# Two graph layers on one core: one-hots from 32-bit lanes, 32-bit rows in the first layer, sums cleared by ScalarE

## The reference, cut to what matters

```python
deg_inv_sqrt = jnp.where(deg > 0, jax.lax.rsqrt(jnp.maximum(deg, 1.0)), 0.0)
out = jax.ops.segment_sum(x[row] * (deg_inv_sqrt[row] * deg_inv_sqrt[col])[:, None], col, num_segments=n)
x = _layernorm(x + out)                       # first layer
h = jax.nn.relu(edge_feat @ W1 + b1)          # 212500 x 64
w = (h @ W2 + b2).reshape(e, 4, 8, 8)
m0 = ALPHA * (s_e*sh0 with w_000  +  C110 * v_e.sh1 with w_110)
m1 = ALPHA * (s_e*sh1 with w_011  +  v_e*sh0 with w_101)
x = _layernorm(x + segment_sum([m0, m1], dst) + SI_SCALE * self_interaction(x))   # second layer
```

## Time and profile before

| | us |
|---|---|
| median of 3 runs | 4708.02 |
| the profiled execution | 4711.18 |
| its span, first to last instruction | 4709.2 |
| PE busy | 2447.2 (52%) |
| PEld busy | 1661.3 (35%) |
| DVE busy | 2178.6 (46%) |
| ACT busy | 795.4 (17%) |
| POOL busy | 3317.1 (70%) |

### The profile page before, as it was taken

The page is one execution under the profiler, slowest core; times in us unless marked ns, Lnnn a source line. Parts: engine busy times, 40 slices in busy tenths (PEclk is TensorE's granted clock), DMA queues, the critical chain, the costliest instruction groups (busy, mean ns, idle before and its releaser), DMA issues.

```text
span 4709.2 us, 30989 instructions
## 1 busy us (share of the span) xinstructions
PE 2447.2 (52%) x10122; PEld 1661.3 (35%) x10122; DVE 2178.6 (46%) x2299; ACT 795.4 (17%) x772; POOL 3317.1 (70%) x3353
## 2 busy tenths in 40 slices
PE   6112122221212212122178888888888888888886
PEld 5111111111111111111165555555555555555555
DVE  8300000000000000000048888888888888888884
ACT  0000000000000000000013333333333333333331
POOL 0577777777777777777727777777777777777770
PEclk7555555555555555555558989999989989899996
DMA  1111111111111111111101111111111111111110
GB/s 34 31 19 19 19 19 19 19 19 19 19 19 19 19 19 19 19 19 19 24 19 29 26 28 29 26 29 28 27 29 26 29 29 26 28 29 26 29 29 16
DMA packets 170010, 112.08 MB, mean 24 GB/s; under 512 B 100473, under 2 KB 154250, under 8 KB 169775
## 3 DMA queue, kind: packets, MB, share of 16 engines
q0 software_dynamic: 106528, 68.39, 10.0%
q1 hardware_dynamic: 63345, 41.87, 3.2%
HBM read 104.41 MB, written 5.61 MB: 23 GB/s over the span
## 4 chain that ended last, share of the span: by engine, by line
POOL 45%; PE 19%; issue 17%; DVE 10%; DMA 7%; ACT 1%; POOLq 0%; DVEq 0%; SPq 0%; ACTq 0%
POOL yg L344 45%; PE ps L477 12%; DMA yg<-scaled_x_table,idx 5%; PE ps L556 4%; DVE msg L899 4%; PE ps L506 2%; DMA yg<-x_table,idx 2%; PE ps L454 1%; DVE prod_all L889 1%; DVE oh L747 1%; DVE prod_all L883 1%; DVE z_sb L645 1%; ACT vec L401 1%; PE ps L549 1%; DVE msg L908 0%
## 5 line engine op out<-in xcount | busy, mean ns | idle before, releaser
L344 POOL DMA_INDIRECT yg<-scaled_x_table,idx x1664 | 1671.5, 1004 | 657.4 <-issue 530.9
L344 POOL DMA_INDIRECT yg<-x_table,idx x1664 | 1635.0, 983 | 612.7 <-issue 520.6
L477 PE MATMUL ps<-oh,yg 128*96 128x144 bf16 x1664 | 455.7, 442 | 1784.8 <-DMA yg<-scaled_x_table,idx 1784.8
L556 PE MATMUL ps<-w2t,hT 128*128 128x256 f32 x3328 | 956.4, 437 | 366.6 <-ACT hT L392 366.6
L760 DVE TENSOR_TENSOR sumT_all<-sumT_all,ps 96x144 f32 (+1 forms) x208 | 61.1, 294 | 2041.3 <-PE ps L477 2041.3
L477 PEld LDWEIGHTS ps<-oh,yg 128*96 128x96 bf16 x1664 | 284.4, 178 | 1955.9 <-DMA yg<-scaled_x_table,idx 1838.4
L556 PEld LDWEIGHTS ps<-w2t,hT 128*128 128x128 f32 x3328 | 673.2, 213 | 803.2 <-ACT hT L392 542.5
L899 DVE TENSOR_REDUCE msg<-prod_all 128x192 f32<-128x1536 f32 x416 | 723.9, 1740 | 0.0
L883 DVE TENSOR_TENSOR prod_all<-ps,feat 128x768 f32<-128x768 f32 x416 | 397.4, 955 | 342.1 <-PE ps L556 275.0
L477 PE MATMUL ps<-ohf,msg 128*64 128x144 f32 x3328 | 473.4, 305 | 8.5 <-DVE msg L908 8.5
L477 PEld LDWEIGHTS ps<-ohf,msg 128*64 128x64 f32 x3328 | 442.2, 148 | 71.2 <-issue 58.6
(11 more groups left out here) (99 smaller groups left out, 705.1 us busy)
## 6 DMA issues: line engine op xcount, KB each, us to landing
yg<-scaled_x_table,idx POOLq DMA_INDIRECT x1664, 2.4
efT<-in_efT SPq DMA_DIRECT2D x104, 256.0 KB
yg<-x_table,idx POOLq DMA_INDIRECT x1664
idx<-in_src SPq DMA_DIRECT2D x208, 8.0 KB, 1.6
sh<-in_sh SPq DMA_DIRECT2D x104, 32.0 KB
scaled_x_table<-sumT_all SPq DMA_DIRECT2D x4, 588.0 KB
x_sb<-in_x SPq DMA_DIRECT2D x1, 1568.0 KB
x_table<-q_sb SPq DMA_DIRECT2D x8, 196.0 KB
```

What stands on the lines that cost most here:

```text
L344: pool.indirect_dma_start(rows[k][:, t, :], None, table, bass.IndirectOffsetOnAxis(ap=idx[k][:, t:t + 1], axis=0),).then_inc(s_g[layer][k] ...
L477: mm = pe.matmul(ps_sum[layer][:, k, :], rows[:, t, :], oh[k][:, :, t] if layer == 0 else ohf[:, t, :], start=(t == 0), stop=(t == TPC - 1))
L556: mm = pe.matmul(ps_w[j % 2][:, t, :], hT[j % 2][:, t * P:(t + 1) * P], w2t[:].rearrange("p c o i -> p (c o i)"), start=True, stop=True)
```

## The change

The split in three parts is dropped. VectorE scales the rows once per quarter, and the table holds 32 values of 32 bits (`y_d`); the gathered rows go to the same buffers in both layers (`xg`), and the first layer's matmuls are 32-bit as the second's. The sum of a chunk is made in two spans of 8 tiles (`SPC`, `TPS`), each 76 lanes wide (`SW`) and with a base of its own, so that the one-hots are 16 x 76 32-bit values from the 32-bit lanes `lane_f` in both layers, and are read by TensorE as they are: ScalarE's conversion (408) goes. `load_bases` reads two registers and `add_sums` makes two additions of 76 columns, the second waiting for the first. ScalarE clears the sums in both layers (`clear_sums`), from a constant zero, in place of VectorE's memsets. In the second layer ScalarE's scalars come after the second rectification, not the first. POOL's warm-up gather and the small identities `parts` are gone.

```diff
@@ -15,8 +15,9 @@
-LW = 144
-D3 = 96
+SPC = 2
+TPS = TPC // SPC
+SW = 76
@@ -62,7 +63,7 @@
-        y_d = nc.dram_tensor("scaled_x_table", (NPAD, D3), BF16).ap()
+        y_d = nc.dram_tensor("scaled_x_table", (NPAD, D), F32).ap()
@@ -70,8 +71,7 @@
-        sumT = [sumT_all[0:D3, :], sumT_all[0:DM, :]]
-        y3 = sumT_all[:, 0:NC * D3 // 2].bitcast(BF16).rearrange("p (c f) -> p c f", f=D3)
+        sumT = [sumT_all[0:D, :], sumT_all[0:DM, :]]
@@ -122,22 +121,18 @@
-        yg = [sb(f"yg{k}", [P, TPC, D3], BF16) for k in range(2)]
-        xg = [yg[k][:].rearrange("p t f -> p (t f)").bitcast(F32)[:, 0:TPC * D].rearrange("p (t f) -> p t f", f=D)
-              for k in range(2)]
+        xg = [sb(f"xg{k}", [P, TPC, D]) for k in range(2)]
...
-        oh = [sb(f"oh{k}", [P, LW, TPC], BF16) for k in range(2)]
-        ohf = sb("ohf", [P, TPC, LW])
+        oh_all = [sb(f"oh{k}", [P, TPC, SW]) for k in range(2)]
+        oh = [[o[:] for o in oh_all]] * 2
...
-        wide_all = prod[0].rearrange("p t b i o -> p (t b i o)")
-        wide_oh = [wide_all[:, 0:WIDE].bitcast(BF16).rearrange("p (t w) -> p t w", t=2),
-                   wide_all[:, 0:2 * WIDE].rearrange("p (t w) -> p t w", t=2)]
+        wide_oh = [prod[0].rearrange("p t b i o -> p (t b i o)")[:, 0:2 * WIDE].rearrange("p (t w) -> p t w", t=2)] * 2
@@ -146,8 +141,8 @@
-        ps_sum = [ps[0:m, 6:8, 0:LW] for m in (D3, DM)]
-        ps_wide = [ps[0:m, 7, :] for m in (D3, DM)]
+        ps_sum = [ps[0:m, 6:8, 0:SPC * SW].rearrange("p k (s w) -> p k s w", s=SPC) for m in (D, DM)]
+        ps_wide = [ps[0:m, 7, :] for m in (D, DM)]
@@ -238,9 +232,9 @@
-                sp.wait_ge(s_split[0], 3 * q + 3)
+                sp.wait_ge(s_scaled, q + 1)
...
-                sp.dma_start(y_v[:, c, :], y3[0:NP, c, :]).then_inc(s_table[0], 16)
+                sp.dma_start(y_v[:, c, :], z_sb[0:NP, c, :]).then_inc(s_table[0], 16)
@@ -320,11 +309,6 @@
-            pool.wait_ge(s_idx[0][0], 16)
-            pool.indirect_dma_start(xg[0][:, 0, :], None, x_d,
-                                    bass.IndirectOffsetOnAxis(ap=idx[0][:, 0:1], axis=0)).then_inc(s_warm, 16)
-            pool.wait_ge(s_warm, 16)
@@ -357,12 +341,13 @@
         def _(act):
...
             act.activation(root[0:NP, :], root[0:NP, :], ACT.Sqrt).then_inc(s_root, 1)
-            for q in range(SPLITS):
-                c = slice(q * SC, (q + 1) * SC)
-                for part in range(2):
-                    act.wait_ge(s_split[0], 3 * q + part + 1)
-                    act.activation(y3[0:NP, c, D * part:D * (part + 1)], z_sb[0:NP, c, :],
-                                   ACT.Copy).then_inc(s_split[1], 1)
+            def clear_sums(layer):
+                act.activation(sumT[layer], zero_b[0:sumT[layer].shape[0], 0:1].to_broadcast([sumT[layer].shape[0], SUMW]),
+                               ACT.Copy).then_inc(s_zero, 1)
...
+            act.wait_ge(s_pool_c, 11)
+            act.wait_ge(s_degree, 1)
+            clear_sums(0)
@@ -401,29 +386,14 @@
                                xg[k][:, :, MUL:D].rearrange("p t (i m) -> p t i m", m=3), ACT.Copy).then_inc(s_scal, 1)
...
-            def one_hots_f32(n):
-                act.wait_ge(s_oh[1], n + 1)
-                if n >= 1:
-                    act.wait_ge(s_sum[1], n)
-                act.activation(ohf[:].rearrange("p t w -> p w t"), oh[n % 2][:], ACT.Copy).then_inc(s_ohf, 1)
...
-            act.wait_ge(s_near, 1)
-            all_near = act.value_load(near[0:1, 0:1], min_val=0, max_val=1)
...
-            def rectified(near_sums):
-                for n in range(CHUNKS):
-                    rectify(GPC * n)
-                    scalars(n)
-                    rectify(GPC * n + 1)
-                    rectify(GPC * n + 2)
-                    rectify(GPC * n + 3)
-                    if near_sums:
-                        one_hots_f32(n)
...
-            with act.If(all_near == 1):
-                rectified(True)
-            with act.Else():
-                rectified(False)
+            act.wait_ge(s_tr[0], PIECES)
+            clear_sums(1)
+            for n in range(CHUNKS):
+                rectify(GPC * n)
+                rectify(GPC * n + 1)
+                scalars(n)
+                rectify(GPC * n + 2)
+                rectify(GPC * n + 3)
@@ -467,15 +437,14 @@
                 k = n % 2
...
-                    pe.wait_ge(s_oh[0], n + 1)
                 else:
                     pe.wait_ge(s_msg, 2 * n + 2)
-                    pe.wait_ge(s_ohf, n + 1)
+                pe.wait_ge(s_oh[layer], n + 1)
...
-                    pe.wait_ge(s_acc[layer], n - 1)
+                    pe.wait_ge(s_acc[layer], SPC * (n - 1))
...
-                    mm = pe.matmul(ps_sum[layer][:, k, :], rows[:, t, :], oh[k][:, :, t] if layer == 0 else ohf[:, t, :],
-                                   start=(t == 0), stop=(t == TPC - 1))
+                    mm = pe.matmul(ps_sum[layer][:, k, t // TPS, :], rows[:, t, :], oh[layer][k][:, t, :],
+                                   start=(t % TPS == 0), stop=(t % TPS == TPS - 1))
                 mm.then_inc(s_sum[layer], 1)
...
             def wide_sums(layer, rows, n, landed):
@@ -497,26 +466,26 @@
-                pe.wait_ge(s_acc[layer], CHUNKS)
+                pe.wait_ge(s_acc[layer], SPC * CHUNKS)
...
                     for c in range(CPP):
...
-                                       parts[0:D3, :] if layer == 0 else places[0:DM, :], start=True, stop=True)
+                                       ident[0:D, 0:D] if layer == 0 else places[0:DM, :], start=True, stop=True)
...
-                    window_sums(0, yg[n % 2], n)
+                    window_sums(0, xg[n % 2], n)
...
-                    wide_sums(0, yg[k], k, (k, 16 * TPC))
+                    wide_sums(0, xg[k], k, (k, 16 * TPC))
...
-                        wide_sums(0, yg[k], 2 * i + k, (k, 16 * TPC * i + 16 * TPC))
+                        wide_sums(0, xg[k], 2 * i + k, (k, 16 * TPC * i + 16 * TPC))
@@ -599,25 +568,25 @@
-            dve.tensor_copy(first_f[:], first_i[:, ::GPC]).then_inc(s_dve_c, 1)
+            dve.tensor_copy(first_f[:], first_i[:, ::GPC // SPC]).then_inc(s_dve_c, 1)
...
-            step(dve.tensor_tensor(rel.rearrange("p (n t) -> p n t", t=TPC),
-                                   dst_f[:].rearrange("p (n t) -> p n t", t=TPC),
-                                   first_f[:].unsqueeze(2).to_broadcast([P, CHUNKS, TPC]), ALU.subtract))
+            step(dve.tensor_tensor(rel.rearrange("p (n t) -> p n t", t=TPS),
+                                   dst_f[:].rearrange("p (n t) -> p n t", t=TPS),
+                                   first_f[:].unsqueeze(2).to_broadcast([P, CHUNKS * SPC, TPS]), ALU.subtract))
...
-            step(dve.tensor_copy(lane[:], lane_f[:, 0:LW].unsqueeze(2).to_broadcast([P, LW, TPC])))
+            step(dve.tensor_copy(lane[:], lane_f[:, 0:NC].unsqueeze(2).to_broadcast([P, NC, TPC])))
...
-            step(dve.tensor_scalar(near_f[:, 0:1], spans[:, 0:1], LW - 0.5, None, ALU.is_le))
+            step(dve.tensor_scalar(near_f[:, 0:1], spans[:, 0:1], SW - 0.5, None, ALU.is_le))
@@ -703,23 +672,10 @@
             dve.wait_ge(s_xin, 16)
...
-            def scaled(q):
+            for q in range(SPLITS):
...
-                                  dinv[0:NP, c].unsqueeze(2).to_broadcast([NP, SC, D]),
-                                  ALU.mult).then_inc(s_split[0], 1)
...
-            def scaled_rest(q, part):
-                c = slice(q * SC, (q + 1) * SC)
-                dve.wait_ge(s_split[1], 2 * q + part + 1)
-                out = z_sb[0:NP, c, :] if part == 0 else y3[0:NP, c, 2 * D:3 * D]
-                dve.tensor_tensor(out, z_sb[0:NP, c, :], y3[0:NP, c, D * part:D * (part + 1)],
-                                  ALU.subtract).then_inc(s_split[0], 1)
...
-            for q in range(SPLITS):
-                scaled(q)
-                for part in range(2):
-                    scaled_rest(q, part)
+                                  dinv[0:NP, c].unsqueeze(2).to_broadcast([NP, SC, D]), ALU.mult).then_inc(s_scaled, 1)
@@ -743,22 +699,25 @@
             def one_hots(layer, n):
                 k = n % 2
...
-                    dve.wait_ge(s_sum[0] if layer == 0 else s_ohf, n - 1)
-                dve.tensor_tensor(oh[k][:], rel_b[:, n * TPC:(n + 1) * TPC].unsqueeze(1).to_broadcast([P, LW, TPC]),
-                                  lane[:], ALU.is_equal).then_inc(s_oh[layer], 1)
...
-            def load_base(n):
...
-                return dve.value_load(first_i[0:1, GPC * n:GPC * n + 1], min_val=0, max_val=n_out)
...
-            def add_sums(layer, n, base):
+                    dve.wait_ge(s_sum[layer], n - 1)
+                dve.tensor_tensor(oh[layer][k], rel_b[:, n * TPC:(n + 1) * TPC].unsqueeze(2).to_broadcast([P, TPC, SW]),
+                                  lane_f[:, 0:SW].unsqueeze(1).to_broadcast([P, TPC, SW]),
+                                  ALU.is_equal).then_inc(s_oh[layer], 1)
...
```

(25 more changed lines are left out.)

36 lines of the change are left out of this document (14 added, 22 removed).

## The result

The changed kernel takes 4665.9 us (median of 4 runs, 4665.0 to 4667.0), the kernel before 4705.9 us beside it: ratio 0.9915, interval 0.990 to 0.993. That is 40 us less, where 101 were forecast; the time is inside the range, but the sum behind it is not met: its two largest terms failed, and the saving on the first gather, which it had at 0, makes up for a part of them.

The account below looks back on a forecast made before the run. POOL's gathers were taken as the bound. Savings of 18.7 (table), 54 and 20 (gathers) and 9 (tail), less 0.5, gave 101.2 us off the profiled 4711.2, hence 4606.8 us at the median; range 4535 to 4705.

Parts of the forecast that it names:

- What bounds the kernel: Whole kernel: POOL's gathers, one after the other, fill nearly the whole span; an undisturbed gather takes 0.94 or 0.95 us.
- The table, -18.7: First layer's table: one product per quarter replaces the split, so POOL starts near 136.3 us; -18.7 us.
- First gather, 0: First layer's first gather, 13.6 us too long: no change taken, range -13.6 to +1 us.
- Rival B: Start of the first layer: the first gather's 13.6 us go with the memset, 4593 us; chance 0.12.
- Gathers of the first layer, -54: First layer: one-hots start 7.64 us after the 16th gather's start; 0.33 us lost a chunk, -54 us.
- Rival A: Both layers: one-hots on the wrong side of the edge, 4802 us; chance 0.05 for both, 0.12 for one edge.
- Gathers of the second layer, -20: Second layer: POOL stays the bound, gathers lose 0.44 us a chunk to VectorE instructions; -20 us.
- ScalarE clears, 0: Clearing of the sums in both layers: at most 20 us each, the first hidden; 0, up to +3 us.
- Tail, -9: After the last gather: 25.6 us to the row conversion instead of 35.0; -9 us.
- Rival C: Gathers of both layers: only the half-width fast form of the one-hots blocks them, 4547 us; chance 0.12.
- Rival D: Second layer: VectorE or TensorE becomes the bound, a chunk takes 20.8 us as now, 4636 us; chance 0.08.
- E: Sums: the narrow path isn't taken and 25 wide windows a chunk make it several times slower; chance 0.01.

Follow-up runs that it names:

- delay and semaphore: Kernel after with a VectorE memset of 1,024 elements ahead of each first-layer chunk's one-hots and a semaphore between the two: 4664.3 us, ratio 0.9904.
- without the semaphore: Kernel after with the same memset ahead of each first-layer chunk's one-hots and no semaphore between them: 4783.1 us, ratio 1.0156, on the same chip.

## Why the prediction came out as it did, point by point

- **What bounds the kernel: right.** The four pieces and their ends account for the change (table above), and the undisturbed gather is 0.94 us in every version. With all held gathers removed, the time is 145 us below after, of 150 us of excess, and nothing else takes its place.
- **The table, -18.7: right**, to the tenth.
- **First gather, 0: wrong, -13.3.** The step said that the memset is no good culprit, since the later memset leaves gathers at 0.94 us, and named the one-hots at 167.45 as perhaps part of it. The observation was right, the value taken from it wrong: it is the two together. Rival B had the size right, with a chance of 0.12, but as the reason only that the memset goes. What the rows said and the step passed over: the gather of the earlier trace rows ends at 169.56, 0.82 us after the *first* of the one-hots behind the memset, and behind the later memset a wait for its semaphore comes first. One thing isn't settled: the long first gather starts 1.8 us ahead of the memset's record and would have been through by then. The trace of before has VectorE's branch, which stands between memset and one-hots, at 154.13 us, and the gather starts at 154.98 (in the run with the memset put back 135.39 and 136.27). So both can have been in VectorE's queue when the gather asked, and a hold that begins with the queueing would fit; that was not tested by itself.
- **Gathers of the first layer, -54: wrong, -9.6.** The mechanism is right (a gather that asks beside the one-hots ends 0.82 us after them; with a PSUM operand none is held). The term that failed is TensorE's 32 passes, taken as 4.8 us "as it has stage and clock in common". From start to addition they took 4.40 us where the clock stayed low (2233.69 to 2238.09), which is the 4.4 that the text had from the 32-bit row and passed over, and 4.04 on average, as the granted clock rises on the way (below). The additions cost 0.51 instead of 0.42. 2.42 + 4.04 + 0.51 = 6.97 instead of 7.64, the wrong side of what the text itself called a knife edge. Beside the mis-sized term there is a mistake in method: with starts that spread over 0.8 us against requests every 1.248, a forecast of 0.33 us a chunk picked a lucky phase. If any phase is as likely as another, a lock as long as the pace or longer catches the one gather that asks first and costs its length less half the pace, 1.41 - 0.62 = 0.79 us a chunk. That estimate would have given 82 us for 88.8, -7 for this term; measured are 0.76 us a chunk. It is no rule, though: in the second layer the one-hots have the same length and cost 0.39. The 0.76 with delay and semaphore is the same phase one gather on and doesn't confirm it. For the 2.19 us without the semaphore (1002.82 to 1005.01) it gives 1.57, and 1.90 was measured, since the memset starts at 7.45 on average, just ahead of the request at 7.62.
- **Rival A** (one-hots ahead of 7.55: 1.3 us lost a chunk) was the side that came true in the first layer, but its price was too high: it took the start just ahead of the request, and it is 0.65 ahead.
- **Gathers of the second layer, -20: wrong, +4.9.** Parts are right: the third product's wait for TensorE is down from 1.84 us to 0.55 at most, the sums take 2.32 us, POOL stays the bound (VectorE waits for landings). The step that failed is the place, 19.8 to 20.4 us after the 16th gather's start. `dots` starts not at 2.42 but at 3.3 on average, as the 16th gather is often held itself (1.15 us on average for 0.94) or VectorE is late, and from there to the next one-hots it is 18.5 us on average instead of 17.3 to 18.0 (the two register loads alone leave a gap of 1.48 us), so the one-hots come at 21.75 on average, and between 20.7 and 24.0 in nine of ten chunks. One chunk:

```profile
3000.94 1.42 DVE L703 TENSOR_TENSOR oh<-rel_b,lane_f 128x1216 f32<-128x1216 bf16 x1
3000.99 2.19 POOL L328 DMA_INDIRECT xg<-x_table,idx  x1 [0.30 <-issue]
...
3004.64 0.56 DVE L824 TENSOR_TENSOR dots<-xg,sh 128x384 f32<-128x384 f32 x1 [2.28 <-DMA xg<-x_table,idx]
...
3007.26 0.96 DVE L838 TENSOR_TENSOR prod_all<-ps,feat 128x768 f32<-128x768 f32 x1 [1.48 <-issue]
```

  By the instruction after whose end each held gather ends, the one-hots cost 0.39 us a chunk where 0.1 was taken, `dots` 0.11 where 0.35 was taken, and the two products of the messages (861, 863), taken as passed by, 0.10 each: 0.70 in all against 0.44, and 0.63 before.
- **ScalarE clears, 0: right.** 10.85 and 10.86 us, and the first ends at 135.84, ahead of the first gather.
- **Tail, -9: -6.3.** From last gather to row conversion 28.8 us (4566.38 to 4595.17), where 25.6 were forecast and 35.0 stood before. The landing is the term that was off, 4.3 us for 2.4 (and 4.3 in before too); the chain took 18.9 for 17.5, sums and addition 4.2 for 4.6, the rest 1.4 for 1.1.
- **Rival C** (only the fast half-width form holds gathers) falls, and with it the inference that the prediction set beside it from the Trainium skill, page "SBUF — State Buffer", section "Who interferes with whom" (a two-input VectorE product leaves descriptor writing alone): the 32-bit one-hots cost 79 us in the first layer, and one operand in PSUM takes them away.
- **Rival D** has the second layer's pace right, 20.8 us a chunk as before (2170.3 / 104 = 20.9), but not by its reason: VectorE waits 93.8 us for landings, so neither it nor TensorE is the bound. **E** did not come.

## What to carry to other kernels

Where a train of indirect gathers sets the time, list the VectorE instructions beside it that read two SBUF operands and put one operand of each in PSUM, rather than work out between which gathers they fall; here that was worth 145 us of 4666. Where such an instruction must stay, don't forecast from a single phase: here a lock of 1.41 us cost a chunk 0.1 to 1.35 us by its phase, and in the first layer the mean over all phases, 0.79, was nearer to the measured 0.76 than the place worked out. Don't let it stand directly behind a memset: one semaphore between the two was worth 119 us.

## What the runs showed of the hardware that was not expected

**A queued instruction shuts gathers out.** A product of two SBUF operands that is next in line behind a memset holds gathers that ask while the memset runs: 13.6 us at the first gather (14.96 against 1.29 with a semaphore between), 1.90 against 0.76 us a chunk in the train. The memset alone doesn't (eight gathers of 0.94 or 0.95 us beside one of 10.72).

**TensorE's clock rises within a chunk's passes.** In the first layer of before the granted clock is 0.50 throughout; in after it averages 0.57, with less TensorE work in the busy column. The first layer of after, then slices of 1 us over the passes that start at 262.27 (busy of PE, PEld, DVE, ACT, POOL, then the granted clock):

```profile
136.00:2316.00 2180.00, 400.68 (x3296) 380.01 (x3296) 181.87 (x308) 0.00 (x0) 1648.67 (x1664) 0.57 0.09 13
...
263.00:264.00 1.00, 1.00 (x10) 1.00 (x9) 0.00 (x0) 0.00 (x0) 0.70 (x2) 0.50 0.10 13
264.00:265.00 1.00, 1.00 (x11) 1.00 (x9) 0.00 (x0) 0.00 (x0) 0.70 (x2) 0.50 0.06 11
265.00:266.00 1.00, 0.95 (x13) 0.77 (x10) 0.00 (x0) 0.00 (x0) 0.74 (x1) 0.91 0.07 16
266.00:267.00 1.00, 0.00 (x0) 0.00 (x0) 0.77 (x3) 0.00 (x0) 0.94 (x1) 1.00 0.16 16
```

The passes run back to back, and part way through them the clock goes from 1.2 to 2.4 GHz, so that the 32 passes take 3.67 us. In the chunk at 2233.69 it stays at 0.50 until the passes are over, and they take 4.26. It rises ahead of the passes' end in 84 of 104 chunks, which take 3.96 us from start to addition on average, and not in the other 20, which take 4.42. That moves the one-hots by up to 0.7 us from chunk to chunk (one takes 1.05 us more than the shortest), which is most of the spread in their starts. In before, TensorE is as busy in a chunk (4.38 us), with 16 longer bf16 passes, and the clock doesn't rise; what makes the difference wasn't tried.
